# Reordering the probability turn, the table load and the last quad of a six-layer local-attention stage

## What is computed

```python
for i in range(DEPTH):                                   # DEPTH = 6
    x = attn_layer(shift_tokens(x), Wqkv[i], ...) + x    # q, k normalised and rotated, band of 32, softmax, @ Wo
    x = ffn_layer(shift_tokens(x), g[i], b[i], W1[i], b1[i], W2[i], b2[i]) + x

def ffn_layer(x, g, bln, W1, b1, W2, b2):
    xn = (x - mu) / sqrt(var + 1e-05) * g + bln
    a, gate = split(xn @ W1 + b1)
    return a * gelu(gate) @ W2 + b2
```

## Time and profile before

| | |
|---|---|
| median of 3 runs (lowest, highest) | 2477.01 us (2473.96, 2479.35) |
| the profiled execution | 2479.06 us, its span 2477.3 us |
| busy in the span | PE 2364.8, DVE 1911.1, ACT 1454.1, POOL 1185.9 us |
| mean granted TensorE clock | 0.988 of full speed |
| instructions | 60785 |

### The profile page before, as it was taken

How to read it: one execution, slowest core, us unless ns; L and a number is a source line. 1 busy time by engine, 2 the same in 40 slices (tenths; PEclk the granted TensorE clock), 3 DMA queues, 4 the chain that set the end, 5 groups by cost and what they waited for, 6 DMA issues and landing times.

```text
span 2477.3 us, 60785 instructions
## 1 busy us (share of the span) xinstructions
PE 2364.8 (95%) x25500; PEld 1430.0 (58%) x25500; DVE 1911.1 (77%) x3471; ACT 1454.1 (59%) x2047; POOL 1185.9 (48%) x883
## 2 busy tenths in 40 slices
PE   6998999999999999999999999978899999999999
PEld 5785656666666666666666666644555555455443
DVE  5889899999999899999999999846866666445222
ACT  2344666666666666666666666634466677566443
POOL 2326777777777777777777777722211111101000
PEclk9999999999999999999999999989899999999999
DMA  4000000000000000000000100002010100120110
GB/s 126 8 7 6 2 2 27 10 8 7 27 10 8 7 27 10 13 2 27 10 13 2 36 2 11 2 1 86 9 38 9 41 28 20 46 87 17 38 54 23
DMA packets 36164, 56.27 MB, mean 23 GB/s; under 512 B 6380, under 2 KB 20852, under 8 KB 35640
## 3 DMA queue, kind: packets, MB, share of 16 engines
q1 hardware_dynamic: 35896, 52.40, 6.8%
HBM read 51.19 MB, written 1.19 MB: 21 GB/s over the span
## 4 chain that ended last, share of the span: by engine, by line
PE 56%; DVE 27%; ACT 12%; issue 5%; POOL 1%; SPq 0%; DMA 0%; DVEq 0%; ACTq 0%
PE w L1392 9%; PE w L1382 9%; DVE turned L979 5%; DVE norm L986 4%; PE w L644 4%; PE w L625 4%; PE w L635 4%; PE py L659 3%; PE w L414 3%; DVE top L430 3%; DVE straight_odd L974 2%; PE w L712 2%; ACT sq L878 2%; PE w L1513 2%; ACT sq L869 2%
## 5 line engine op out<-in xcount | busy, mean ns | idle before, releaser
L425 ACT ACTIVATE prob<-logit 128x512 f32<-128x512 f32 x224 | 137.6, 630 | 278.8 <-DVE logit L433 278.8
L1382 PE MATMUL w<-qT,m_fc 128*128 128x512 f32 x544 | 267.8, 605 | 0.4 <-ACT turned L1631 0.4
L1129 POOL TENSOR_TENSOR straight_odd<-straight_odd,turned 128x1024 f32<-128x1024 f32 x96 | 227.3, 2369 | 82.9 <-DVE turned L979 80.1
L455 POOL TENSOR_TENSOR prob<-prob,rden 128x1024 f32<-128x1024 f32 x112 | 213.5, 1906 | 68.4 <-DVE rden L444 68.4
L979 DVE TENSOR_TENSOR turned<-w,rot 128x512 f32<-128x512 f32 x384 | 245.3, 680 | 0.0
L1129 POOL TENSOR_TENSOR straight<-straight,turned 128x1024 f32<-128x1024 f32 x96 | 226.5, 2369 | 37.3 <-DVE turned L979 37.3
L1123 POOL TENSOR_TENSOR straight_odd<-straight_odd,rnorms 128x1024 f32<-128x1024 f32 x96 | 180.5, 1902 | 115.8 <-DVE rnorms L1000 115.8
L986 DVE TENSOR_REDUCE norm<-sq 128x16 f32<-128x1024 f32 x192 | 224.1, 1208 | 0.0
L1123 POOL TENSOR_TENSOR straight<-straight,rnorms 128x1024 f32<-128x1024 f32 x96 | 180.4, 1899 | 70.0 <-DVE rnorms L1000 70.0
L474 POOL TENSOR_TENSOR fresh_roots<-fresh_means,eps 128x1 f32<-128x1 f32 x64 | 12.1, 190 | 379.1 <-DVE fresh_means L462 379.1
L891 ACT COPY qT<-w 128x1024 f32<-128x1024 f32 x96 | 97.3, 1013 | 162.4 <-PE w L671 162.4
(11 more groups left out here) (253 smaller groups left out, 5295.9 us busy)
## 6 DMA issues: line engine op xcount, KB each, us to landing
b_wqkv<-gates SPq DMA_DIRECT2D x64, 256.0 KB, 3.7
b_wqkv<-in_b_wqkv SPq DMA_DIRECT2D x18, 512.0 KB, 3.5
ctxT<-in_ctxT SPq DMA_DIRECT2D x64, 64.0 KB, 1.8
b_wo<-in_b_wo SPq DMA_DIRECT2D x6, 512.0 KB, 3.5
m_fc<-in_m_fc SPq DMA_DIRECT2D x1, 2304.0 KB, 9.4
m_proj<-in_m_proj SPq DMA_DIRECT2D x1, 2304.0 KB, 13.0
m_fc<-in_m_fc SPq DMA_DIRECT2D x8, 256.0 KB, 3.4
m_proj<-in_m_proj SPq DMA_DIRECT2D x8, 256.0 KB, 3.4
```

The lines of the kernel that those rows point to most:

```text
L455: pool.tensor_tensor(flat, flat, k.rden[:, s, :, None].broadcast_to([P, HEADS, SEQ]), ALU.mult).then_inc(k.prob_ready, 1)
L1129: pool.tensor_tensor(k.straights[s][:, i, :, :], k.straights[s][:, i, :, :], k.turned[:, i, :, :], ALU.add).then_inc(added, 1)
L1382: pe.matmul(claim(("hidden", J, c)), k.m_fc[:, x, c * P:(c + 1) * P], k.m_xT[:, q, :], start=True, stop=True).then_inc(k.ring_full, 1)
```

## The change

Three edits. Where a step has no hidden layer, PE turns the probabilities in front of the queries, and ACT copies them in front of the queries; in a hidden step their place is as before. In a hidden step ACT runs `affine` in front of the first table load and `gelu` 0 in front of the copy of the values. The last quad, 23, gets buffers and banks of its own (`w1`, and parts of `xs`, `kT`, `qT`, `v2`) and is turned in and normalised in step 99, hidden in step 100 and put out in step 102; the loop ends with step 102. The banks of `turn_out` alternate between `w0` and `w2`.

```diff
+LAST_STEP = 6
+LAST_QUAD = {TURN: 3, NORMALISE: 3, HIDDEN: 4, OUTPUT: 6}
 def quad_at(g, lag):
+    if g == STEPS + LAST_QUAD[lag]:
+        return ALL_QUADS - 1
     Q, r = divmod(g - lag, 4)
-    return Q if not r and 0 <= Q < ALL_QUADS else None
+    return Q if not r and 0 <= Q < ALL_QUADS - 1 else None
+
+def line_bank(k, Q):
+    return k.w1[:, 512:1024] if Q == ALL_QUADS - 1 else k.py[:, :]
+def gate_bank(k, Q):
+    return k.w1[:, 0:512] if Q == ALL_QUADS - 1 else k.pt[:, :]
+def quad_buffers(k, Q):
+    return (k.xs2, k.xnT2, k.gate2, k.hid2) if Q == ALL_QUADS - 1 else (k.xs[:, 0, :, :], k.xnT, k.gate, k.hid)
+def back_bank(k, q):
+    return (k.w0, k.w2)[q % 2]
...
     def quad_in(Q):
         pe.wait_ge(k.row_added, 2 * Q + 2)
-        if Q:
+        if Q == ALL_QUADS - 1:
+            pe.wait_ge(k.shifted, FIRST + STEPS)
+        elif Q:
...
     def turn_out(q):
-        w = (k.w0, k.w1, k.w2, k.w0)[q]
+        w = back_bank(k, q)
         pe.wait_ge(k.unshifted, q + 1)
-        if q == 3:
-            pe.wait_ge(k.back_added, 1)
+        if q > 1:
+            pe.wait_ge(k.back_added, q - 1)
...
 # PE
         if hid is not None:
             hidden(hid, 0, g)
+        if before2 and hid is None:
+            turn_probs(g - 2, before)
         if before and g >= 1:
             turn_queries(g - 1, this)
         if hid is not None:
             hidden(hid, 1, g)
-        if before2:
-            turn_probs(g - 2, before)
+            if before2:
+                turn_probs(g - 2, before)
...
 # ACT
         if hid is not None:
+            affine(hid)
             act.preload_act_table_set("gelu_and_others")
-            affine(hid)
         if this and not is_cross(g):
             ... act.activation(k.sq[:, 1, :, :], k.w1[:, :], ACT.Square)
+        if hid is not None:
+            gelu(hid, 0)
         if before:
             ... act.copy(k.v2[:, 1 - s, :, :], k.w2[:, :])
...
-        if hid is not None:
-            gelu(hid, 0)
+        if before2 and hid is None:
+            turned_probs(g - 2)
         if before and g >= 1:
             ... act.copy(k.qT[:, 1 - s, :, :], k.w0[:, :])
         if hid is not None:
             gelu(hid, 1)
-        if before2:
-            ... act.copy(k.probT[:, :, :], k.w2[:, :])
+            if before2:
+                turned_probs(g - 2)
...
 # DVE
+        if g == STEPS + LAST_QUAD[TURN]:
+            dve.wait_ge(k.o_psum, FIRST + STEPS)
+            dve.memset(k.hid2[64:P, 2, :], 1.0)
+            quad_stats(ALL_QUADS - 1)
         if hid is not None:
             gate(hid, 0)
+        if g == STEPS + LAST_QUAD[TURN]:
+            quad_normalise(ALL_QUADS - 1)
```

More of the change, by code:

```diff
@@ L734, in hidden @@
         at, n = CHUNKS[c]
+        xnT = quad_buffers(k, Q)[1]
         if c == 0:
@@ L738, in hidden @@
             pe.wait_ge(k.row_added, pairs_before(g))
-            pe.wait_ge(k.z_fed, quads_before(g, OUTPUT))
+            if Q < ALL_QUADS - 1:
+                pe.wait_ge(k.z_fed, quads_before(g, OUTPUT))
         else:
             pe.wait_ge(k.gated, 3 * Q + c)
-        pe.matmul(k.pt[0:n, :], k.c_w1[:, HID + at:HID + at + n], k.xnT[:, :], start=True,
+        pe.matmul(gate_bank(k, Q)[0:n, :], k.c_w1[:, HID + at:HID + at + n], xnT[:, :], start=True,
                   stop=True).then_inc(k.gate_psum, 1)
@@ L745, in hidden @@
             pe.wait_ge(k.hid_ready, 3 * Q + c)
-        pe.matmul(k.py[0:n, :], k.c_w1[:, at:at + n], k.xnT[:, :], start=True, stop=True).then_inc(k.line_psum, 1)
+        pe.matmul(line_bank(k, Q)[0:n, :], k.c_w1[:, at:at + n], xnT[:, :], start=True, stop=True).then_inc(k.line_psum, 1)
     def output(Q, g):
@@ L769, in layers_tensor @@
     pe.wait_ge(k.loaded, 16 * N_URGENT)
-    for g in range(-TILES, STEPS + OUTPUT + 1):
+    for g in range(-TILES, STEPS + LAST_STEP + 1):
         this, before, before2 = stages_of(g)
@@ L844, in gelu @@
         act.wait_ge(k.gate_psum, 3 * Q + c + 1)
-        act.activation(k.gate[0:n, c, :], k.pt[0:n, :], ACT.Gelu, bias=k.c_cols[0:n, 5 + c:6 + c]).then_inc(k.gated, 1)
+        act.activation(quad_buffers(k, Q)[2][0:n, c, :], gate_bank(k, Q)[0:n, :], ACT.Gelu, bias=k.c_cols[0:n, 5 + c:6 + c]).then_inc(k.gated, 1)
     def unshift(q):
@@ L856, in turned_x, with turned_probs @@
         act.copy(k.xT[:, g % 2, :], k.pt[:, 0:P]).then_inc(k.xT_ready, 1)
+    def turned_probs(g):
+        act.wait_ge(k.pT_psum, FIRST + g + 1)
+        act.copy(k.probT[:, :, :], k.w2[:, :]).then_inc(k.pT_ready, 1)
     act.preload_act_table_set("natural_log_exp_and_others")
     turned_x(-TILES)
-    for g in range(-TILES, STEPS + OUTPUT + 1):
+    for g in range(-TILES, STEPS + LAST_STEP + 1):
         T, s = FIRST + g, g % 2
@@ L1001, in refine_norms, with feed @@
                                  op1=ALU.mult).then_inc(k.newton_step, 1)
-    def feed(first, n):
-        cols = k.py[:, 0:n * SEQ].rearrange("p (b n) -> p b n", n=SEQ)
+    def feed(bank, first, n):
+        cols = bank[:, 0:n * SEQ].rearrange("p (b n) -> p b n", n=SEQ)
         low, high = k.z[0:64, first:first + n, :], k.z[64:P, first:first + n, 1:SEQ]
@@ L1087, in layers_vector @@
             dve.wait_ge(k.row_psum, p + 1)
-            feed(4 * p % (2 * TILES), 4).then_inc(k.row_added, 1)
+            feed(k.py, 4 * p % (2 * TILES), 4).then_inc(k.row_added, 1)
         if out is not None:
             dve.wait_ge(k.out_psum, out + 1)
-            feed(8 * out % (2 * TILES), 8).then_inc(k.z_fed, 1)
-        if quad_at(g, TURN) is not None:
+            feed(line_bank(k, out), 8 * out % (2 * TILES), 8).then_inc(k.z_fed, 1)
+        if quad_at(g, TURN) is not None and g < STEPS + LAST_QUAD[TURN]:
             quad_stats(quad_at(g, TURN))
-        if quad_at(g, NORMALISE) is not None:
+        if quad_at(g, NORMALISE) is not None and g < STEPS + LAST_QUAD[TURN]:
             quad_normalise(quad_at(g, NORMALISE))
```

24 lines of the change are left out of this document (13 added, 11 removed).

## The result

The changed kernel takes 2450.66 us (median of 4 runs, 2445.9 to 2452.6) against 2475.49 us for the kernel before on the same chip; the ratio is 0.9896, 95% interval 0.9875 to 0.9916. It is faster by 1.0%, 24.8 us, where 27 were forecast. The profiled execution took 2452.6 us with a span of 2450.8 us, 26.5 less than before.

What follows compares the result with a forecast made beforehand. PE was taken to bound the layers, idle only 27.3 us there, with DVE close behind. The terms 19.1 + 1.7 - 0.6 + 7.1 = 27.3 us, off the median 2477.01, gave 2450, range 2440 to 2461.

Steps and rivals of the forecast that it cites:

- case A: Whole kernel: the chain of waits holds as followed, 2450 us, by itself 2444 to 2455; chance 0.68.
- the hidden step: 22 steps with hidden layer: affine and gelu 0 earlier on ACT bring `turn_keys` forward, 0.87 each, 19.1 us.
- the last quad: Tail: quad 23 turned in and normalised during quad 22's hidden layer, 7.1 us gained; 4.4 at half clock, at best 9.
- The lower bound of that term: 22 hidden steps: if the gelu gives nothing, PE's own wait of 0.41 still goes, 9.0 us.
- rival B: Hidden steps give only the affine wait, PE held at `turn_keys` as before: gain 17.2, time 2460 us; chance 0.13.
- The load: Hidden step on ACT: 1.28 us table load hidden behind key matmuls; drain before last quad's gelu 0 would make 27.3 into 25.9.
- Probabilities first: Even steps: wait moves from attend to scores, 0.07 of 0.27 left, counting one step in four, 1.7 us gained.
- The early steps: Steps 3, 5, 7, 9: PE waits 2.0 before its turns; 0.2 lost in each of three, 0.6 us.
- rival C: Half clock in steps 5, 7, 9 and in the tail: gain 19.6, time 2457 us; chance 0.08.
- E: Slower: PE waits for the late value copy in all 74 steps without hidden layer; at 0.45 each 2483 us; chance 0.04.
- D: Layers and tail: steps where DVE leads shorten too, gain 37, time 2440 us; chance 0.06.
- the value copy: ACT's copy, 0.6 us later in hidden steps, judged covered; releasing PE in steps 12 to 95 would prove the prediction wrong.

Runs made afterwards that it cites:

- Experiment 3: Kernel before with only affine put in front of the table load in the hidden step: 2476.27 us, ratio 1.0005.
- experiment 1: Kernel before with only the probabilities turned and copied in front of the queries in steps without hidden layer: 2475.32 us, ratio 1.0001.
- experiment 9: Changed kernel with probabilities back behind the queries, both ScalarE edits and the last quad's edit kept: 2447.07 us, ratio 0.9880.
- experiment 6: Changed kernel with probabilities in front of the queries only from step 10 on: 2447.05 us, ratio 0.9885.
- experiment 7: Changed kernel with two unused matmuls in front of the turned probabilities in steps 3, 5, 7 and 9: 2445.72 us, ratio 0.9878.
- experiment 5: Kernel before with only the last quad's edit, quad 23 beside quad 22: 2467.92 us, ratio 0.9970.
- experiment 4: Kernel before with only gelu 0 put in front of the value copy, affine still behind the table load: 2468.95 us, ratio 0.9971.
- 10: As experiment 6, but the even step right in front of the hidden one also keeps the old order: 2445.67 us, ratio 0.9879.
- Experiment 8: As experiment 6, with the last two of eight rows matmul pairs put behind `turn_keys` in even steps: 2444.91 us, ratio 0.9873.

## Why the prediction was right, term by term

The forecast was 2450, by case A, and the time is 2450.66. The sum was 27.3 us; the spans differ by 26.5 and the medians by 24.8. That the time was met within 0.7 us is in part luck: the sum was 2.5 us too large against the medians, and the kernel before stood at 2475.49 beside the changed one, 1.5 us below the 2477.01 from which the forecast was reckoned. The interval of the ratio allows any gain from 21 to 31 us. The terms were less good than the total: the hidden step carried the forecast, the first edit gave nothing measurable, and in the last quad 1.4 us that I had not counted met 1.4 us lost to the clock.

**The hidden step: 0.87 forecast, 0.90 measured with these edits alone, 0.79 in the full change.** The chain as followed is there: `turn_keys` moved by 0.78 where I had 0.83, and PE arrives there as the turned keys do (DVE's rotation starts 5.71 behind the start of the keys and takes 1.28, and PE's eight probability turns, from 6.13 at 0.87, end at 7.00). 19.8 us were to be had by the steps (22 x 0.90), 19.2 were measured, 19.1 forecast. In the full change it is 22 x 0.79 = 17.4, because the first edit takes 0.1 back.

**The lower bound of that term, and rival B, were wrong.** I held that if gelu 0 gave nothing, the affine edit would still give PE's own wait, 0.41 x 22 = 9.0. Experiment 3 gives 0, with an interval whose lower end is 0.9995: 1.2 us at most. The earlier trace rows already held the reason: PE waits at L683 for the rotation, ready at 1374.16 + 1.28 = 1375.44, so an earlier gate pair only lengthens that wait. I had said that a wait that goes on one engine must go on the other too, and did not apply it to the bound. With 0 in place of 9.0, rival B would have stood at 2469 and not at 2460.

**The load was called hidden behind the key matmuls.** It is not hidden on ACT. In the changed kernel it stands in that unbroken queue, and DVE waits for the gelu at its end. So the 1.28 us lie on the chain to DVE's first gate whenever PE leads, by these rows (no run took the load away); the square "kept its place" only because the affine gave the load its own. The load is followed by the square 0.01 after its end again (1352.42 + 1.28, then 1353.71). The load in front of gelu 0 of the last quad, the one that was to tell 27.3 from 25.9, shows no drain either. The gelu starts 0.02 behind it, and 0.14 behind the end of its gate pair (1642.83 + 1.12), where 0.15 was forecast:

```profile
1642.79 1.28 ACT L908 ACT_TABLE_LOAD   x1
1644.09 0.69 ACT L875 ACTIVATE qT<-w,c_cols 128x512 f32<-128x512 f32 x1
```

So 27.3 was the right sum of the two.

**Probabilities first: 1.7 forecast, 1.1 to 1.3 by the step means, with the wrong reason.** The size per step was right (0.07 forecast, 0.05 to 0.06 measured): the copies go back to back on ACT and the wait moves from attend to scores. The even step of the changed kernel shows it, and answers to the earlier trace rows:

```profile
1344.77 1.16 PE L418 MATMUL w<-probT,v 64*64 64x64 f32 x64
...
1344.95 1.03 ACT L934 COPY kT<-w 128x1024 f32<-128x1024 f32 x1
...
1346.03 0.41 PE L728 MATMUL w<-band,ident 64*64 64x512 bf16 x4
```

`attend` no longer waits, and the scores begin 0.05 behind the end of the `kT` copy. But I had it count in one step of four, by who leads. It counts in three of four, and 0.1 of the 0.16 is lost again in the hidden one. That leaves 0.06 a period, 59.65 - 59.59, in experiment 1 and 0.05, 58.75 - 58.70, between experiment 9 and the changed kernel, or 1.1 to 1.3 us in 21 periods. The early steps below take more than that. The lead of one engine is no gain until the engines that follow it have it too.

**The early steps: 0.6 forecast, 0.8 measured in steps 5, 7 and 9, and half clock in one of the three.** The 2.02 us of idle time stand where they were predicted, in front of the turned probabilities. The changed kernel's step 5, to be held against the earlier trace rows:

```profile
272.14 1.09 PE L717 MATMUL w<-ident,prob 128*128 128x128 f32 x8 [2.02 <-ACT v L917]
...
276.17 0.41 PE L728 MATMUL w<-band,ident 64*64 64x512 bf16 x4
```

The step lost 0.28 where I had 0.2. Of rival C a third came true: step 9 fell to half clock (eight turns in 1.88 to 1.90 us against 1.04) and cost 1.58, as reckoned (1.6). Step 3 ran at half clock before and after (its turned probabilities took 1.82 after). In the profile of the change the early steps as a whole (3, 5, 7, 9) moved by -0.39 + 0.28 + 0.28 + 1.86 = +2.0 us, more than the swap gave in all the steps behind them. Experiments 6 and 7 confirm the first half: without the swap there, 12.80; with it and PE kept busy, 13.08. The clock is less settled. The forecast read half clock from the one 2.42 of step 3, but that gap lowered the clock in seven kernels of nine only (last section).

**The last quad: 7.1 forecast, 8.4 alone, 6.8 in the full change.** The start of `turn_out(0)` before, then the tail after, answering to the earlier trace rows:

```profile
1661.59 0.27 PE L764 MATMUL w<-ident,m_proj 64*128 64x64 f32 x1 [0.58 <-ACT turned L852]
```

```profile
1632.47 1.06 PE L750 MATMUL w<-ident,m_proj 128*128 128x128 f32 x4
...
1637.23 1.36 DVE L1060 TENSOR_SCALAR xs<-w,mv,rstd 128x128 f32<-128x128 f32 x4
...
1640.90 0.27 PE L792 MATMUL w<-ident,m_proj 64*128 64x64 f32 x1 [0.47 <-ACT turned L882]
...
1641.30 0.66 PE L756 MATMUL w<-ident,xs 128*128 128x128 f32 x4
...
1642.83 1.12 PE L770 MATMUL w<-kT,c_w 128*128 128x512 f32 x2 [0.87 <-ACT kT L869]
...
1648.58 2.74 PE L781 MATMUL py<-hid,c_w 128*128 128x512 f32 x6
...
1651.16 2.74 PE L781 MATMUL w<-v,c_w 128*128 128x512 f32 x6
...
1657.05 0.75 DVE L1076 TENSOR_TENSOR x_all<-x_all,w 128x256 f32<-128x256 f32 x2 [0.21 <-PE w L793]
```

Quad 23 is turned in and normalised while quad 22 is in its hidden layer, and `quad_turn` follows `turn_out(0)` by 0.40 (1641.30 - 1640.90) instead of 6.58 (1668.17 - 1661.59): 6.2, where 6.1 were forecast. From `quad_turn` to quad 23's output are 9.86 us, forecast 9.65, before 10.73; but the terms of the forecast, 10.73 + 2.65 - 1.0 - 2.7 + 0.15, make 9.83, so the terms together were right and their addition was 0.2 off. The end is 0.25 longer, forecast 0.1. What I had not counted is quad 22's own hidden layer: the turning of quad 23 now stands in front of its gate and line matmuls. Of these, three groups of six ran at a lower clock before, and they took 8.47 us from their start to `turn_out(0)` (1653.12 to 1661.59); now one group does (2.07), and they take 7.35. With 0.27 gained in front of them that is 1.4 more. From quad 22's normalising to the merged stage the gain is 6.2 + 1.4 + 0.9 - 0.3 = 8.2 us. The clock in it is no accident of one execution: in all five profiles with the old tail three groups of each of the two quads ran wholly or in part at the lower clock, and in all seven with the new one at most two of quad 22 and none of quad 23, which is the full clock that was forecast. Which part of the new order does it was not tested. In the full change 1.4 of it is given back ahead of that point, where PE's clock was lower in that execution (0.66 from 1612 to 1632 us): the last rows matmuls took 6.67 us there and 6.05 in experiment 5. So the tail is not a fixed sum either; between the kernels with the last quad changed it took 73.13 (experiment 9) to 75.67 us (the changed kernel).

**The other rivals.** E, slower through the value copy in all 74 steps, did not happen. The forecast had named the value copy as a releaser of PE in steps 12 to 95 as a sign of being wrong, and it shows up: one weight load waits for it 21 times in the layers, 0.3 us at most, once in each step with an output layer. No matmul waits for it, and the three steps without a hidden layer are each shorter than before. D did not happen either, and B only in experiment 4, without the affine edit.

The parts alone gave 2475.4 - 2475.3, 2475.4 - 2456.2 and 2475.3 - 2467.9, in sum 0.1 + 19.2 + 7.4 = 26.7 us; the whole gave 24.8, which the intervals do not tell apart. So the second edit gives about seven tenths of the gain, the third the rest, and the first nothing that can be measured. The four kernels that keep the second and third edits and leave out, delay or cover the first (experiments 6, 7, 9, 10) stand at 2445.7 to 2447.1, 3.6 to 5 us below the changed kernel; their ratios, 0.9878 to 0.9885, lie within its interval. The 94 steps (1374.7 to 1377.2 against 1377.65) say the same for up to 3 us of it; the rest is the tail and the merged stage, which vary between executions by as much (788.5 to 793.0 in the profiles). Experiment 8 has the lowest median, 2444.91, 30.4 us below the kernel before; experiments 7 and 10 lie within 1 us of it.

## What to carry to other kernels

A bound for "only this edit" must be followed to the next wait: removing 0.41 us of a matmul engine's idle time was worth nothing while the same engine waited for the vector engine a few groups of matmuls later, and two edits worth 0 and 0.37 alone were worth 0.90 together. When engines follow each other as closely as here, most of a lead won by one engine in three steps is given back in the fourth where another sets the pace; add up a whole period before multiplying. A reorder that helps the steady steps should be switched off in the steps of the start-up that lack the work it hides behind, or the gap filled.

## What the runs showed of the hardware

Idle time of the same length in front of the same eight turns lowered TensorE's clock in some steps and not in others. Each count here is of one profiled execution a kernel.

| idle time in front of the turns | where | fell to the lower clock |
|---|---|---|
| 2.42 | step 3, the nine kernels with the old order there | 7 of 9; not in experiments 4 and 6 |
| 2.02 | steps 3, 5, 7 and 9, changed kernel and experiment 1 | 3 of 8: steps 3 and 9 of the changed kernel, step 5 of experiment 1 |
| 1.00 (once 1.45) | steps 5, 7 and 9, the nine kernels | none of 27 |
| 0.30 | steps 3, 5, 7 and 9, experiment 7 | none of 4 |

Where the clock fell, a row of eight turns behind the gap took up to 1.97 us, against 1.04 to 1.10 at full clock. The clock granted for 200 to 330 us was 0.97 in the changed kernel and in experiment 1, 1.00 in experiment 6 and 0.99 in experiment 7 and before. What decided it in these steps was not settled, and so a single step at the lower clock, as the forecast had it, is weak ground for a price.
